# Sort stage of a graph kernel: the rank selection in 16-bit integers, GpSimd's spread in two released parts, 17 of 26 one-hot rows on ScalarE

## What is computed

```
edge_index = jnp.stack([src, dst])
h = relu(layernorm(x));  x = x + L0(h, edge_index, weight)
h = relu(layernorm(x));  x = x + L1(h, edge_index, edge_attr_4, ...)
# both: h[src], h[dst] per edge, then jax.ops.segment_sum(message, src, N)
```

## Time and profile before

| what | value |
|---|---|
| median of three executions | 14280.81 us (14270.75 to 14292.7) |
| profiled execution, time | 14276.82 us |
| its span, first to last instruction | 14275.1 us |
| mean granted TensorE clock, of full speed | 0.689 |
| first start of L668, last start of L668 | 326.2 us, 2843.3 us |
| busy over the span: POOL, DVE, PE, ACT | 68%, 57%, 41%, 30% |

### The profile page before, as it was taken

How to read it: one execution, slowest core, us unless ns; L and a number is a source line. 1 busy time by engine, 2 the same in 40 slices (tenths; PEclk the granted TensorE clock), 3 DMA queues, 4 the chain that set the end, 5 groups by cost and what they waited for, 6 DMA issues and landing times. The chain is left out here.

```text
span 14275.1 us, 194787 instructions
## 1 busy us (share of the span) xinstructions
PE 5915.9 (41%) x49303; PEld 4889.8 (34%) x49304; DVE 8192.2 (57%) x17300; ACT 4286.9 (30%) x8244; POOL 9668.0 (68%) x10331
## 2 busy tenths in 40 slices
PE   3555555511111111111178633333333333388998
PEld 3555555411101111111168622222222222236997
DVE  6999999933343334334388844444444444467887
ACT  1888888800000000000078600000000000053334
POOL 0666666677777777777767557777777777704774
PEclk6777777755555555555599866666666666699999
DMA  2000000033333333333334323322322232274332
GB/s 68 9 9 9 9 9 9 9 88 89 87 84 91 88 88 87 87 89 86 81 122 140 101 71 81 82 81 80 82 82 79 82 82 81 78 248 128 104 105 76
DMA packets 1108753, 1129.16 MB, mean 79 GB/s; under 512 B 667728, under 2 KB 807632, under 8 KB 1108432
## 3 DMA queue, kind: packets, MB, share of 16 engines
q1 hardware_dynamic: 819920, 661.83, 16.7%
q0 software_dynamic: 228864, 241.63, 8.6%
q10 hardware_dynamic: 59904, 224.95, 4.0%
HBM read 848.31 MB, written 279.45 MB: 79 GB/s over the span
## 5 line engine op out<-in xcount | busy, mean ns | idle before, releaser
L1645 POOL DMA_INDIRECT big<-b_d,big x3328 | 3179.5, 955 | 1195.9 <-issue 966.1
L1112 POOL DMA_INDIRECT big<-h_d,big x3328 | 3210.6, 965 | 1024.6 <-issue 962.2
L1166 PE MATMUL ps<-big 128*128 x3328 | 634.4, 371 | 3578.1 <-PEq L159 3565.8
L1166 PEld LDWEIGHTS ps<-big 128*128 128x128 bf16 x3328 | 483.3, 152 | 3729.0 <-issue 3725.8
L1719 PE MATMUL ps<-big 128*128 x3328 | 559.9, 319 | 2765.6 <-PEq L159 2765.1
L1197 DVE TENSOR_TENSOR HA<-big 128x1024 f32<-128x1024 f32 x208 | 254.8, 1225 | 2477.6 <-DVEq L159 2476.2
L1317 PE MATMUL ps<-big 128*128 128x130 f32 (+1 forms) x6656 | 1460.1, 301 | 179.6 <-issue 178.6
L1719 PEld LDWEIGHTS ps<-big 128*128 128x128 bf16 x3328 | 420.2, 146 | 3082.2 <-issue 3077.9
L1758 DVE TENSOR_TENSOR big<-ps,big 128x1024 f32<-128x1024 f32 x208 | 254.6, 1224 | 2002.5 <-DVEq L159 2002.5
L1971 POOL TENSOR_SCALAR big<-iota_f,big 128x128 f32<-128x128 f32 x1456 | 850.1, 604 | 814.7 <-DMA big<-rec_d 494.0
L800 ACT ACTIVATE big<-big 128x512 bf16<-128x512 bf16 x1984 | 1228.9, 707 | 288.9 <-ACTq L159 288.9
(11 more groups left out here) (409 smaller groups left out, 14567.1 us busy)
## 6 DMA issues: line engine op xcount, KB each, us to landing
big<-e_d SPq DMA_DIRECT2D x416, 512.0 KB, 3.2
rows_d<-big ACTq DMA_DIRECT2D x208, 544.0 KB, 2.8
big<-rows_d SPq DMA_DIRECT2D x208, 544.0 KB, 3.4
HA<-slots_d SPq DMA_DIRECT2D x208, 512.0 KB, 3.7
big<-slots_d SPq DMA_DIRECT2D x208, 512.0 KB
e_d<-big ACTq DMA_DIRECT2D x208, 512.0 KB
big<-rec_d SPq DMA_DIRECT2D x832, 64.0 KB, 3.2
big<-h_d,big POOLq DMA_INDIRECT x3328
```

The source lines that it names most:

```text
L1112: gp.indirect_dma_start(G[g][:, t * ROW:(t + 1) * ROW], None, h0_d, bass.IndirectOffsetOnAxis(idx[g][:, t:t + 1], 0)).then_inc(gath[g], 16)
L1166: m = t.matmul(XS[h][:, n, 0:3 * D + 3], OT3[g % 2][:, o, :], T0x[:, ds((chunks[o // 2] + steps[o // 2]) * TW if o % 2 else chunks[o // 2] ...
L1645: gp.indirect_dma_start(G[g][:, t * D:(t + 1) * D], None, b_d, bass.IndirectOffsetOnAxis(idx[g % 2][:, t:t + 1], 0)).then_inc(gath[g], 16)
```

## The change

The selection moves from float32 to 16-bit integers. `A2` becomes an int16 tile in SBUF, padded from 99 to `NCP` = 100 columns per half (the padding column is zeroed once), `B` gets 100 columns per edge, and `prod` is int16. The sum along the chunks is made in two steps: the second half of each edge's 100 products is added to the first half (int16, 1,300 elements), and `tensor_reduce` sums the 50 that are left. The small tiles between count and place (`n_i`, a new `n_r`, `sel`, `q_i`, `sg_i`, `l_i`) move from SBUF to PSUM.

```
-        prod = take(J * NC)
+        prod = take(J * NCP // 2, I16)
-        A2 = ps[:, 2048:2048 + 2 * NC].rearrange("p (g c) -> p g c", g=2)
+        A2f = take(NCP, I16)
+        sel = ps[:, 2592:2592 + J]
+        q_i, sg_i, l_i = (ps[:, 2624 + n * 32:2624 + n * 32 + J].bitcast(I32) for n in range(3))
+        n_i, n_r = (ps[:, 2048 + n * 128:2048 + n * 128 + NC].bitcast(I32) for n in range(2))
```

```
+                    if not first:
+                        n = targets(1 - b)
+                    need(n)
+                    v.sem_inc(l_rdy, 1)
+                    if not last:
+                        ranks(1 - b)
...
+                    spread_pieces(0, 8)
+                    consume(gp, l_rest)
                     gp.tensor_tensor(EX4[b][:, :, 0:3, :], PC[:, ds(s * J, J), :].unsqueeze(3).to_broadcast([P, J, 3, L]),
                                      OHL[b].unsqueeze(2).to_broadcast([P, J, 3, L]), ALU.mult).then_inc(e_done, 1)
+                    spread_pieces(8, 12)
+                    consume(gp, e_done, 3)
```

On ScalarE `ACTD` goes from 16 to 17, so VectorE makes 9 one-hots, and the 16 Relus of 512 elements become two, of 4,608 and 4,096:

```
-        ACTD = 16
+        ACTD = 17
+        HALF = (ACTD + 1) // 2
...
-                    for n in range(ACTD):
-                        j = J - ACTD + n
-                        a.wait_ge(s_sq, n + 1)
-                        o = DH[b][:, j * WS:(j + 1) * WS]
+                    for n, m in ((0, HALF), (HALF, ACTD)):
+                        a.wait_ge(s_sq, m)
+                        o = DH[b][:, (J - ACTD + n) * WS:(J - ACTD + m) * WS]
```

More of the change, by code:

```diff
@@ L11 @@
 U16 = mybir.dt.uint16
+I16 = mybir.dt.int16
 ALU = mybir.AluOpType
@@ L435, in build @@
         wp = [take(J) for _ in range(2)]
-        sel, seg_f = take(J), [take(J) for _ in range(2)]
-        q_i, sg_i, l_i = (take(J, I32) for _ in range(3))
+        seg_f = [take(J) for _ in range(2)]
         stage = [take(NW * L * REC) for _ in range(2)]
@@ L492, in build @@
         s_c, s_sq = sem("so_chain"), sem("so_square")
-        b_rdy, rt_rdy, l_rdy, s_piece, d_rdy, da_rdy, e_rdy, y_rdy, st_rdy, seg_rdy = (
-            sem(f"so_{k}") for k in ("b", "rt", "l", "piece", "d", "da", "e", "y", "st", "seg"))
+        b_rdy, rt_rdy, l_rdy, l_rest, s_piece, d_rdy, da_rdy, e_rdy, y_rdy, st_rdy, seg_rdy = (
+            sem(f"so_{k}") for k in ("b", "rt", "l", "lrest", "piece", "d", "da", "e", "y", "st", "seg"))
         scat = sem("so_scat")
@@ L596, in _ @@
                 v.memset(ANC[:, 0:1], 0.0)
+                v.memset(A2f, 0.0)
                 v.memset(ps[:, 2560 + J:2561 + J], 0.0)
@@ L644, in before, with ranks, targets @@
                     m = same.rearrange("p (g m) -> p g m", g=2)
-                    n = go(v.tensor_tensor(m, m, earlier.unsqueeze(1).to_broadcast([P, 2, GJ * GJ]), ALU.mult))
-                    need(n)
+                    return go(v.tensor_tensor(m, m, earlier.unsqueeze(1).to_broadcast([P, 2, GJ * GJ]), ALU.mult))
+                def ranks(b):
                     go(v.tensor_reduce(wp[b], same.rearrange("p (j k) -> p j k", k=GJ), AX, ALU.add))
-                def take_out(b):
+                def targets(b):
                     consume(v, y_rdy)
@@ L675, in supertile @@
                     need(a2)
[L676 to L677 removed]
                     n = go(v.tensor_tensor(prod.rearrange("p (g j c) -> p g j c", g=2, j=GJ),
                                            B[b].rearrange("p (g j c) -> p g j c", g=2, j=GJ),
[L680 removed]
+                                           A2.unsqueeze(2).to_broadcast([P, 2, GJ, NCP]), ALU.mult))
                     need(n)
[L682 removed]
+                    need(go(v.tensor_tensor(prod3[:, :, 0:NCP // 2], prod3[:, :, 0:NCP // 2],
+                                            prod3[:, :, NCP // 2:NCP], ALU.add)))
+                    if not first:
+                        v.sem_inc(l_rest, 1)
+                    need(go(v.tensor_reduce(sel, prod3[:, :, 0:NCP // 2], AX, ALU.add)))
                     need(go(v.tensor_tensor(q_i, sel, wp[b], ALU.add)))
@@ L710, in supertile @@
                     need(n)
-                    go(v.tensor_tensor(dest[b], dsum, g8, ALU.add))
+                    n = go(v.tensor_tensor(dest[b], dsum, g8, ALU.add))
+                    if not first:
+                        n = targets(1 - b)
[3 more added lines that the diff above has]
+                        ranks(1 - b)
                     if not first:
@@ L718, in _ @@
                 flags(0, 0)
-                before(0, 0)
+                need(before(0, 0))
+                ranks(0)
                 supertile(0, 0, first=True)
@@ L726, in _ @@
                 supertile(1, NS - 1, last=True)
-                v.sem_inc(l_rdy, 1)
+                v.sem_inc(l_rest, 1)
+                need(targets(1))
                 take_out(1)
```

39 lines of the change are left out of this document (22 added, 17 removed).

## The result

The changed kernel takes **14073.26 us**, median of four executions (14072.27 to 14078.35). Its ratio to the kernel before is 0.986, 95% interval 0.9848 to 0.9872, against a median of 14277.9 us of four executions of that kernel. The profiled execution took 14074.02 with a span of 14072.3, against 14276.82 and 14275.1 before.

The account below looks back on a forecast made before the run. VectorE was taken to set the pace at 20.46 us a supertile; its terms gave 18.75, and waits 19.23, so 1.23 less over 123 periods and about 2 for the last supertile: 14128 us, range 14025 to 14235.

Parts of the forecast that it names:

- that case's own range: Range of the main case, VectorE setting the pace with waits for GpSimd and TensorE of 0.1 to 0.9; chance 0.58.
- product to L699 (before: L678 to L683), 5.74: VectorE's selection: 16-bit product and halving at 0.52 ns an element, then the sum; 3.95 us in place of 5.74.
- late scatter DMA, three times: GpSimd's scatter DMA sometimes starts 2.7 us late and no longer has slack; +0.06 us a supertile.
- counts to product, with two tiles in PSUM: Two VectorE instructions ahead of the product move to PSUM, 0.26 us in place of 0.21 for 99 elements; +0.10 in all.
- five small instructions: Five VectorE instructions of 26 elements, moved to PSUM, cost 0 to 0.05 us more each; taken as +0.05 in all.
- one one-hot less: VectorE makes nine one-hots in place of ten; a tenth of 2.72 us is saved, -0.27.
- `targets` before `l_rdy`: On VectorE `targets` must finish before `l_rdy` is given, so L655's 0.17 us no longer overlaps; +0.17.
- wait of `flags` for GpSimd's last part: VectorE's `flags`, with two SBUF inputs, waits for the end of GpSimd's second spread part; +0.17 us, bounded by 0 and 1.59.
- wait for TensorE's ranks: `place` and `ranks` give `rt_rdy` late in some supertiles; VectorE waits up to 1.0 us, +0.25 on average.
- First part: GpSimd's 1,664-element spread starts about R + 13.3, ends R + 16.3, 0.1 to 0.5 us before the product; R starts sum L698.
- The slow 16-bit rate: Rival: product and halving add run at 1.04 ns an element, 2.03 us more a supertile, 14380 us; chance 0.08.
- ScalarE as the bound: Rival: no wait comes up, the scatter's brush with the one-hots shrinks, ScalarE's 18.3 us a supertile decides, 14015 us; chance 0.12.

Follow-up runs that it names:

- the releases behind the issue: Changed kernel with four semaphore releases on VectorE each put behind the issue of the next instruction; 14066.38 us, ratio 0.9856.
- the float version: Changed kernel with the selection back in float32, A2 in PSUM, one sum over 100 columns; split spread and 17 one-hots stay; 14300.49 us, ratio 1.0021.
- ScalarE's part alone: Kernel before, with 17 one-hots on ScalarE in place of 16 and two wide Relus; 14223.38 us, ratio 0.9969.
- two edits of 8 us each: Changed kernel with four releases behind the next issue (14066.38 us), or TensorE's totals first with their own semaphore (14065.54); with both, 14019.27.

## Why the prediction was right, and where it was off

The forecast was 14128 with a range of 14025 to 14235; the time lies inside, 55 below the forecast and 7 below that case's own range. (That range is stated as 14080 to 14185; with its terms, waits of 0.1 to 0.9, it begins at 14088.) The order of events came as laid out: VectorE runs almost without a pause, `rt_rdy` becomes late in some supertiles, ScalarE and GpSimd stay just hidden. But VectorE is not the bound alone, as the sum has it: with its own order 0.94 shorter the period hardly fell. The ring through TensorE and GpSimd, 18.81, is about as long as VectorE's own sum (18.73 without the wait for TensorE). The prediction had the ring as a wait only, and that the two lengths nearly coincide is luck for its sum. The sum was 1.23 a supertile; it is 1.63. Term by term, with mean times from start to start over the stage:

| term | forecast | measured |
|---|---|---|
| product to L699 (before: L678 to L683), 5.74 | -1.79 | -1.67 |
| late scatter DMA, three times | +0.06 | +0.08 |
| counts to product, with two tiles in PSUM | +0.10 | +0.04 |
| five small instructions | +0.05 | +0.01 |
| `flags`, 26 elements more | +0.03 | +0.03 |
| one one-hot less | -0.27 | -0.40 |
| sum moved from `before` to `ranks` | 0 | -0.11 |
| `targets` before `l_rdy` | +0.17 | +0.25 |
| wait of `flags` for GpSimd's last part | +0.17 | 0 |
| wait for TensorE's ranks | +0.25 | +0.11 |
| where the rows go, L721 to L666 | 0 | +0.04 |
| sum (the period itself: -1.63) | -1.23 | -1.62 |

- **Selection.** The rate was read rightly from L645. The 0.12 that is missing is the release: from the halving to the sum 0.98 pass, and 0.87 where the release stands behind the issue of the sum. I had put 0.03 there. The Trainium skill (Vector Engine (DVE) Microarchitecture Reference, section 5.1) sets two-byte operands and a step of one as the condition for two elements a cycle; the trace agrees for bf16 times int16 (1.50 for 2,600) and for int16 alone (0.84 for 1,300).
- **One-hots.** The term failed in size, by 0.13: I took a tenth of ten undisturbed one-hots. The last of the ten took 0.68 to the next start, stretched by a scatter DMA; the last of the nine takes 0.55. The prediction named this brush among the arguments of a rival and left it out of its sum.
- **`flags`.** No wait: it takes 2.87, the 2.84 of before and 26 elements more. I had the second part last from R + 0.30 to R + 3.09 and `flags` start at R + 2.92. Measured: R + 0.21 to R + 2.98, because the release stands 0.11 ahead of the sum, and `flags` at R + 2.89; that they overlap by 0.09 in the trace without a price lies within the roughness of GpSimd's spans. With the releases behind the issue `flags` starts 2.62 behind the sum and takes 3.19 in place of 2.87: the lock was there, just missed.
- **TensorE.** Forecast: pair of 10.1 to 11.9, `rt_rdy` at R + 13.8 to 15.6. Measured: 10.2 and 11.2 in turn, so `rt_rdy` at R + 13.9 and 14.9. The difference is TensorE's clock: behind 8 us without matmuls the first group of `place` runs at a granted clock of 0.50 in both kinds; over the second group it is 0.82 in one kind (1504.9 to 1506.5) and still 0.50, all at 1.2 GHz, in the other (1523.3 to 1525.8), and its 26 matmuls take 1.80 and 2.79. Only every other supertile waits, 0.22 longer, and I had taken more than twice that on average.
- **GpSimd.** First part at R + 12.93 against 13.3 forecast, without a pause, ended just before the product. The spare is 0 and 0.9 in turn. Where a scatter DMA is late, the price is the whole lock:

```profile
1435.91 2.98 POOL L875 TENSOR_TENSOR big<-big 128x1664 bf16<-128x1664 bf16 x1 [0.37 <-POOLq L160]
1436.01 4.26 DVE L690 TENSOR_TENSOR big<-HA,big 128x2600 int16<-128x2600 bf16 x1
```

Three products of 124 look so, 2.76 too long each, as the three gaps of the earlier trace rows led to expect.

- **The rivals.** The slow 16-bit rate fell with the first row. ScalarE as the bound was closer than its chance of 0.12 says: with 18 one-hots or narrow Relus it is the bound (its floor is 17.9 where the prediction has 18.3; its terms there add up to 18.1 before the start). The slower outcome that the prediction did not have is the lock at the small instructions: I counted the PSUM tiles as a cost of 0.15 and did not ask what they were for. With the four small ones back in SBUF the gain is 61 us, and the selection without split and tiles is a loss of 201. The prediction was right there only because the change already held the cure.

What stays open: the 0.6 a supertile that the split costs in the float version can be placed by its trace beside that of ScalarE's part alone. 0.13 is the release ahead of the sum (3.00 from the product's start for 2.87), 0.11 `targets` and the moved sum together, 0.14 L718 to L724, 0.08 the one-hots, and the rest in steps of 0.06 and less. Why L718 and the one-hots take longer was not separated; GpSimd's attributes, which run beside L718, took longer too (the first 0.58 for 0.37). Nor was the kernel run with the PSUM tiles and the spread in one piece, so how much of the cure is the split and how much the tiles is not shown.

## What to carry to other kernels

Before an operand moves from PSUM to SBUF to gain a rate, list each VectorE instruction that then has two SBUF inputs, however short, and what GpSimd does at that moment; one operand left in PSUM took it out of the lock here. Where several engines stand within half a microsecond of each other, look for the ring that they form, and take something from each member: two edits of 8 us each gave 55 together here, with one more wait moved out of the way. Count an engine that may become the bound by its spacing from start to start while it runs without a pause, not by durations plus a start.

## What the hardware showed unexpectedly

- An add of 26 elements took 1.47 us in place of 0.19, by the placement of its tiles alone, and 2.72 beside the spread in one piece; a sum of 1,300 elements with one input ran beside the same GpSimd instruction undisturbed (1.51).
- A release between the end of one VectorE instruction and the issue of the next cost 0.11 us (0.98 against 0.87), a wait for a semaphore long given 0.14 (0.53 against 0.39).
- ScalarE's start of 0.3 us behind a release is not paid when its next work is released before it ends: 18 Squares and two wide Relus repeat every 18.9 us.
